# One attention and feed-forward block on one core: the steady steps in another order

## What is computed

```
x = x + tanh(g_xattn) * (context @ (Wv @ Wout) + bout)          # for these shapes
h = layernorm(x); s1 = 127 / max|h|;  h = round(h * s1) @ round(w1)  -> dequantised + b1
h = gelu(h)
h = layernorm(h); s2 = 127 / max|h|;  h = round(h * s2) @ round(w2)  -> dequantised + b2
x = x + tanh(g_ffn) * h
```

## Time and profile before

| | |
|---|---|
| median of 3 runs | 415.7 us (414.34 to 415.91) |
| the profiled execution, its own time | 413.45 us |
| its span, first to last instruction | 411.7 us |
| mean granted TensorE clock | 0.893 of full |
| busy: PE, DVE, ACT, POOL | 315.3, 299.3, 274.2, 268.2 us |

### The profile page before, as it was taken

How to read it: one execution, slowest core, us unless ns; L and a number is a source line. 1 busy time by engine, 2 the same in 40 slices (tenths; PEclk the granted TensorE clock), 3 DMA queues, 4 the chain that set the end, 5 groups by cost and what they waited for, 6 DMA issues and landing times. The chain is left out here.

```text
span 411.7 us, 5770 instructions
## 1 busy us (share of the span) xinstructions
PE 315.3 (77%) x1661; PEld 201.2 (49%) x1690; DVE 299.3 (73%) x520; ACT 274.2 (67%) x443; POOL 268.2 (65%) x298
## 2 busy tenths in 40 slices
PE   2976827759798989797979797989897666665553
PEld 2855516343556565555555554656464434332232
DVE  0168395978788989797979798979798858565710
ACT  2113672666878887878787888969695959594220
POOL 4052669386878887878787888787777868484100
PEclk9998987997989998989999999989898969695785
DMA  7665213325385756566665657490707161715173
GB/s 236 240 247 191 61 49 83 102 50 130 83 176 121 184 124 158 139 144 139 144 151 131 160 123 178 106 201 28 154 27 153 53 127 52 129 52 103 62 127 94
DMA packets 97974, 51.56 MB, mean 125 GB/s; under 512 B 86567, under 2 KB 88800, under 8 KB 97942
## 3 DMA queue, kind: packets, MB, share of 16 engines
q1 hardware_dynamic: 97046, 51.14, 50.6%
q10 hardware_dynamic: 896, 0.04, 0.1%
HBM read 21.78 MB, written 8.41 MB: 73 GB/s over the span
## 5 line engine op out<-in xcount | busy, mean ns | idle before, releaser
L343 POOL TENSOR_TENSOR y<-u,g_bc 128x1024 f32<-128x1024 f32 x64 | 151.4, 2368 | 41.5 <-ACT u L512 40.9
L681 DVE TENSOR_TENSOR y<-y,slot_c 128x1024 f32<-128x1024 f32 x64 | 77.8, 1216 | 47.3 <-PE slot_c L929 31.5
L968 PE MATMUL bank_f<-w2T,q2T 128*128 128x256 f16 x512 | 78.8, 308 | 9.9 <-DMA q2T<-q 7.6
L685 DVE TENSOR_REDUCE amax<-y 128x1 f32<-128x1024 f32 x64 | 77.6, 1213 | 1.8
L493 ACT ACTIVATE q<-y,scale 128x1024 f16<-128x1024 f32 x64 | 69.9, 1142 | 12.8 <-DMA q2T<-q 9.7
L520 ACT ACTIVATE junk<-u,usum 128x1024 bf16<-128x1024 f32 x64 | 73.5, 1149 | 2.1
L968 PEld LDWEIGHTS bank_f<-w2T,q2T 128*128 128x128 f16 x512 | 55.7, 109 | 29.9 <-issue 10.2
L512 ACT ACTIVATE u<-slot_a,d 128x1024 f32<-128x1024 f32 x32 | 35.4, 1107 | 38.3 <-PE slot_a L957 38.3
L929 PE MATMUL slot_c<-ln_rows,rows 128*128 128x512 bf16 x112 | 41.7, 447 | 16.2 <-ACT rows L503 8.9
L904 PE MATMUL slot_a<-wvo,ctxT 128*128 128x256 f32 x208 | 51.4, 380 | 0.0
L726 DVE SCALAR_TENSOR_TENSOR res<-bank_f,d,x 128x256 f32<-128x256 f32 x64 | 27.8, 476 | 19.2 <-PE bank_f L971 19.2
(11 more groups left out here) (113 smaller groups left out, 449.6 us busy)
## 6 DMA issues: line engine op xcount, KB each, us to landing
c_in<-in_ctx SPq DMA_DIRECT2D x16, 512.0 KB, 5.0
x_in<-in_x SPq DMA_DIRECT2D x16, 512.0 KB, 3.5
out<-res SPq DMA_DIRECT2D x32, 256.0 KB, 2.0
y<-in_L_ffn_w SPq DMA_DIRECT2D x2, 1024.0 KB, 9.1
u<-in_L_xattn_Wkv SPq DMA_DIRECT2D x2, 512.0 KB, 6.2
u<-in_L_xattn_Wout SPq DMA_DIRECT2D x2, 512.0 KB, 7.5
q2T<-q SPq DMA_TRANSPOSE x64, 3.3
g_bc<-in_L_ffn_ln_g SPq DMA_DIRECT2D x1, 512.0 KB, 4.5
```

The costliest lines, as they stand in the source:

```text
L343: nc.gpsimd.tensor_tensor(y[:, k % 3, t, :], u[:, t, :], g2_bc[:, :], ALU.mult).then_inc(gain2_done, 1)
L681: nc.vector.tensor_tensor(line, line, slot_c[:, :], ALU.add).then_inc(y_done, 1)
L685: nc.vector.tensor_reduce(amax[:, 1, t:t + 1], y[:, k % 3, t, :], AX.X, ALU.max, apply_absolute_value=True).then_inc(amax2_done, 1)
L968: nc.tensor.matmul(acc, q2T[:, t, j, :], w2T[:, j, :], start=(j == 0), stop=False)
```

## The change

No instruction is added or removed, and none changes its operands. The bodies of four engines are written in another order; POOL's stays.

- PE: `turn_context(i+3, 0)` moves from the head of body i to the end of the body before, `turn_context(i+3, 1)` behind `hidden(3)`. `second_product(i-3, 2)` goes ahead of `turn_rows`, `second_product(i-3, 3)` behind `correction(0)`, and `hidden(0)` follows at once; each later `hidden` has a `correction` ahead of it, and `second_product(i-2, 0)` goes ahead of `hidden(2)`. Half of the attention comes before `second_product(i-2, 1)`.
- ACT: tile 2 is quantised with tiles 0 and 1, ahead of the gelus; tile 3 stays behind the squares, where now the second half of the context is taken first. The first half is taken ahead of `take_rows`.
- DVE: `join` before the rows, `final(i-3, 2)` and `final(i-3, 3)` behind the first row.
- SP: the transpose of tile 2 a body earlier, behind `load_context`, and `store(i-2, 0)` behind it.

```diff
@@ SP
                 if live(i - 3):
-                    store(i - 3, 0)
-                    turn_second(i - 3, 2)
                     turn_second(i - 3, 3)
                 if live(i):
                     turn_first(i)
+                if live(i - 2):
+                    turn_second(i - 2, 0)
                 if live(i + 4) and i + 4 > 1:
                     load_x(i + 4)
+                if live(i - 2):
+                    turn_second(i - 2, 1)
+                if live(i - 3):
+                    store(i - 3, 1)
                 if live(i + 5) and i + 5 > 2:
                     load_context(i + 5)
                 if live(i - 2):
-                    turn_second(i - 2, 0)
-                    turn_second(i - 2, 1)
-                if live(i - 3):
-                    store(i - 3, 1)
+                    turn_second(i - 2, 2)
+                    store(i - 2, 0)
@@ ACT
-                    take_rows()
-                if 0 < i <= S:
-                    take_rows()
                 if live(i + 3) and i > 0:
                     take_context(i + 3, 0)
+                if 0 <= i <= S:
+                    take_rows()
                 if live(i - 2):
                     quantise(i - 2, 0)
                     quantise(i - 2, 1)
+                    quantise(i - 2, 2)
...
                 if live(i + 3) and i > 0:
                     take_context(i + 3, 1)
                 if live(i - 2):
-                    quantise(i - 2, 2)
                     quantise(i - 2, 3)
@@ DVE
+                    join(i + 2)
                 if live(i - 1):
                     row(i - 1, 0)
-                    if live(i + 2):
-                        join(i + 2)
-                    row_max(i - 1, 0)
...
                 if live(i - 3):
                     final(i - 3, 2)
                     final(i - 3, 3)
                 if live(i - 1):
+                    row_max(i - 1, 0)
+                    row(i - 1, 1)
@@ PE
-                if live(i + 3):
-                    turn_context(i + 3, 0)
+                    turn_context(4, 0)
+                if live(i - 3):
+                    second_product(i - 3, 2)
                 if i <= S + 1:
                     turn_rows()
                 if live(i - 1):
                     correction(i - 1, 0)
-                if live(i + 3):
-                    turn_context(i + 3, 1)
                 if live(i - 3):
-                    second_product(i - 3, 2)
+                    second_product(i - 3, 3)
+                if live(i):
+                    hidden(0)
...
                     hidden(3)
+                if live(i + 3):
+                    turn_context(i + 3, 1)
                 if live(i + 1):
                     shift_first(i + 1)
+                if live(i + 3):
+                    attention(i + 3, 0)
                 if live(i - 2):
-                    second_product(i - 2, 0)
                     second_product(i - 2, 1)
                 if live(i + 3):
-                    attention(i + 3, 0)
                     attention(i + 3, 1)
+                if live(i + 4):
+                    turn_context(i + 4, 0)
```

More of the change, by code:

```diff
@@ L549, in body @@
                     quantise(i - 2, 1)
+                    quantise(i - 2, 2)
+                if live(i):
+                    gelu(0)
+                    square(0)
+                    gelu(1)
+                    square(1)
+                    gelu(2)
+                    square(2)
+                    gelu(3)
+                    square(3)
                 if live(i + 3) and i > 0:
                     take_context(i + 3, 1)
-                if live(i):
-                    for t in range(T):
-                        gelu(t)
-                        square(t)
                 if live(i - 2):
-                    quantise(i - 2, 2)
                     quantise(i - 2, 3)
@@ L786, in body @@
                     statistics(i + 2, 3)
+                    join(i + 2)
                 if live(i - 1):
                     row(i - 1, 0)
-                    if live(i + 2):
-                        join(i + 2)
-                    row_max(i - 1, 0)
-                    row(i - 1, 1)
-                    row_max(i - 1, 1)
-                    if i == S:
-                        scales(slice(1, 2), slice(0, 2))
-                    row(i - 1, 2)
-                    row_max(i - 1, 2)
                 if live(i - 3):
@@ L801, in body @@
                 if live(i - 1):
+                    row_max(i - 1, 0)
+                    row(i - 1, 1)
+                    row_max(i - 1, 1)
+                if i == S:
+                    scales(slice(1, 2), slice(0, 2))
+                if live(i - 1):
+                    row(i - 1, 2)
+                    row_max(i - 1, 2)
                     row(i - 1, 3)
@@ L1030, in body @@
                 if live(i):
-                    hidden(0)
+                    hidden(1)
                 if live(i - 1):
                     correction(i - 1, 2)
+                if live(i - 2):
+                    second_product(i - 2, 0)
                 if live(i):
-                    hidden(1)
-                if live(i - 3):
-                    second_product(i - 3, 3)
+                    hidden(2)
                 if live(i - 1):
@@ L1040, in body @@
                 if live(i):
-                    hidden(2)
                     hidden(3)
+                if live(i + 3):
+                    turn_context(i + 3, 1)
                 if live(i + 1):
                     shift_first(i + 1)
+                if live(i + 3):
+                    attention(i + 3, 0)
                 if live(i - 2):
-                    second_product(i - 2, 0)
                     second_product(i - 2, 1)
                 if live(i + 3):
-                    attention(i + 3, 0)
                     attention(i + 3, 1)
+                if live(i + 4):
+                    turn_context(i + 4, 0)
             for i in bodies:
```

## The result

The changed kernel takes **390.19 us** (median of 4 runs, 389.86 to 393.29), the one before 415.81 us beside it: a ratio of 0.9401 with a 95% interval of 0.9348 to 0.9454. The profiled execution of the changed kernel is its slowest, 393.29 us with a span of 391.5; so the two traces differ by 20.2 us of span where the medians differ by 25.6.

The account below looks back on a forecast made before the run. A loop of waits through PE, ACT, POOL and DVE, no full engine, was taken to set the step. Savings of 14.9, 3.8, 1.4, 0.8 and 4.3 make 25.2 us off 413.45: 388.2, raised to 390; range 382 to 401.

Parts of the forecast that it names:

- The way from rows to gelu: PE and ACT, rows to first gelu: first product can start at T+6.63 (T: last square's end), 1.02 us sooner.
- The step: Steady step by the loop's sum, DVE's work or PE's work: 18.3 us, taken as 18.5, ends 17.7 and 19.6.
- The clock: PE in steady steps: full clock, since no single wait is over half a microsecond.
- rival A: Clock still falls in every steady step: 1.15 us each on eleven steps, 402 us; chance 0.14.
- rival B: Tile 2's q2T transpose lands late behind the context load, delaying `turn_rows`: 5.5 us over eleven steps, 396 us; chance 0.17.
- my own signs of being wrong: Steady steps: PE waits for q2T, clock averages 0.92, or a new wait over 1 us ahead of `hidden(0)`.
- Rival C: Tile 3's q2T transpose lands late ahead of `hidden(0)`: 7 us slower at a 6.5 us landing, 423 us; chance 0.03.
- Ten steps: From `quantise_first` of step 3 to that of step 13: 199.9 us become 185, saving 14.9 us.
- Fill: Steps 1 and 2: first product no longer behind the wait of `correction(1)`; 1.6 and 2.2, together 3.8 us saved.
- Step 13: Step with a nearly full PE before it: 19.9 becomes 18.5, 1.4 us saved.
- Late steps: Steps 14 and 15: clock falls anyway, only `correction(1)` leaves the path; 0.4 a step, 0.8 us saved.
- The drain: Program end: earlier tile 2 transpose 1.5, one last product instead of two 1.9, less tile 3 waiting 0.9; 4.3 us.

Follow-up runs that it names:

- the experiment with the queue turned: Tile 2's transpose put ahead of the context load, against the changed kernel with scales first and first-half store behind tile 3's transpose: 381.31 us, ratio 0.9148.
- the kernel with only the drain undone: Changed kernel, with tile 2's transpose of steps 14 and 15 back behind the first-half store: 392.22 us, ratio 0.9437.
- the last one: Changed kernel with scales first, store behind tile 3's transpose, tile 2's transpose ahead of the context load, and fills in bodies 14 to 18: 378.18 us.

## Why the prediction was right, point by point

**The way from rows to gelu.** Rows, correction and `row(0)` stand at T+4.46 to T+5.85, as in the earlier trace rows, to a hundredth of a microsecond. Tile 3's product starts at T+5.91 (5.65 by the sum), and the first product waits for q1T (forecast 0.2 to 0.3 us, shown 0.4). So `gelu(0)` starts at T+8.78, where the loop's sum has 8.5. Undoing two of the moves cost 0.45 and 0.58 us a step, as worked out; on the kernel before, the same product's move costs time.

**The step**: 18.3 by the sum, shown 18.27 to 18.3 where nothing disturbs it. The loop is the right one, but that its sum is right to a hundredth is luck. The scales ended 20.59 us behind T (20.44 counted), the first w1 product came 5.18 behind them (4.85), `gelu(0)` 1.28 behind that (1.50), and from there to the last square's end it was 9.57 (9.83, since no gelu waited for its product). The four errors cancel. The 0.2 that I added for crossings that I could not resolve was not there. The three ways to the sum were not of equal worth: DVE's and PE's idle times are small because they wait for the loop, and with the scales sooner the step goes to 18.02. I had also called DVE the busiest engine of both steps; in the slow-clock one PE is, with 18.17 us.

**The clock** stayed at 1.00 in the steady steps but one, as forecast, and rival A fell. But the reason that I gave, that no single wait is over half a microsecond, is not shown to be the cause. Filling the idle stretch of the kernel before keeps the clock; yet in the kernel with tile 2's product put back the stretch is idle for 1.28 us, and the clock stays too, as it does in the kernel before with the one move, where PE waits 1.31 and 0.87 us in a step and the context turn stands where it stood. With the load of x first, it held behind one wait of 2.54 us and fell behind another. What exactly lets it fall stays open.

The one step in which it did not stay is this, in the changed kernel's trace: the step, a DMA queue and the q1T transpose in its first microseconds, and PE at the first product and behind it:

```profile
162.01:183.54 21.53, 18.31 (x101) 11.29 (x100) 17.60 (x31) 16.86 (x27) 15.83 (x17) 0.92 0.66 135
...
q8 instruction: 1, 0.02, 1.7%
...
q1T<-q SPq DMA_TRANSPOSE x1, 4.9
...
168.91 0.59 PE L963 MATMUL slot_a<-w1T,q1T 128*128 128x512 f16 x2 [2.43 <-DMA q1T<-q]
...
170.16 1.06 PE L935 MATMUL slot_c<-ln_rows,rows 128*128 128x512 bf16 x2
```

The transpose landed 4.9 us after its issue in place of 3.1, PE waited 2.43 us, the clock went to 1.2 GHz behind it (granted 0.50 from 170 to 173 us), and the step took 21.5 us, 3.2 too long. This execution is 3.1 us above the median. In the kernel before q1T had 0.75 us or more to spare. The kernel with the late fills has the same order up to this step; there q1T landed after 4.5 us, PE waited 2.03 us, the clock stayed at 1.00 and the step took 19.72 us. So of the 3.2 us I estimate 1.4 to 1.8 for the wait, and the rest for the clock.

I overlooked what was in flight beside the late transposes. In both traces one packet of 0.02 MB on DMA queue 8, which the profile calls "instruction", moved within 5 us of the issue of this q1T. It is the same with tile 2 of the changed kernel: of its nine transposes behind a context load three have no such packet beside them and landed after 4.2 to 4.3 us; six have one and landed after 4.7 to 6.2, and five of these six are the ones that PE waited for in the steady steps. No transpose that SP issued singly in the trace of the changed kernel landed after more than 4.5 us without such a packet. Not every packet goes with a late landing, and no run moves the packets, so that they are the cause is not shown.

**SP's queue, rival B.** I had 0.1 to 2.3 us over for tile 2 and counted nothing. The trace shows five waits of PE for tile 2 in steady steps, of 0.19 to 0.85 us, 2.9 us in all; the experiment with the queue turned gives 1.5 us on medians. That is under the 5.5 us of its price. But "PE waits for q2T in steady steps" was one of my own signs of being wrong, and it came; so did, in the disturbed step alone, a wait of over 1 us ahead of `hidden(0)`. The third, a clock of 0.92 in the steady steps, did not. Rival C did not come: tile 3 landed in time until the scales went ahead of the results and pushed the store. Then it did bite, by 0.2 to 0.3 us a step.

**Ten steps**: 14.9 forecast, 13.2 in the trace with the disturbed step and 16.4 without its 3.2; 15.6 in the kernel with only the drain undone, whose ten steps are the same. **Fill**: 3.8 forecast, 3.2 shown, but not where I had it: between starts of `quantise_first` step 1 gave 0.2 us (1.6 forecast), step 2 gave 2.7 (2.2 forecast), and 0.3 were there ahead of step 1. **Step 13**: 1.4 forecast, 1.9 shown.

**Late steps**: 0.8 forecast for two, 0.02 shown for step 14. The term that failed is the clock's: I kept the time at which it comes back as in the kernel before, and it came back later, at 320.3, 5.8 us behind the first correction (4.1 before). The fills show what the clock costs there: 2.45 us in step 14.

**The drain**: 4.3 forecast, with step 15 1.9 shown and 1.9 undone. The 1.9 of the last product came: in the changed kernel PE is left with one. The other two terms, 1.5 and 0.9, failed. The rows are SP, ACT and PE of the changed kernel, and between them (397.24) PE of the kernel before at the product that answers to 377.37:

```profile
370.41 0.34 SPq L230 DMA_DIRECT2D out<-res  x1
370.84 4.04 SPq L224 DMA_TRANSPOSE q2T<-q  x3
...
374.27 1.15 ACT L495 ACTIVATE q<-y,scale 128x1024 f16<-128x1024 f32 x1 [3.49 <-DMA q2T<-q]
...
397.24 1.05 PE L968 MATMUL bank_f<-w2T,q2T 128*128 128x256 f16 x8 [0.97 <-DVE res L726]
...
377.37 1.89 PE L974 MATMUL bank_f<-w2T,q2T 128*128 128x256 f16 x8 [0.97 <-DVE res L732]
...
385.97 1.87 PE L974 MATMUL bank_f<-w2T,q2T 128*128 128x256 f16 x8 [2.45 <-DMA q2T<-q]
```

Measured from the start of step 15 (350.07 before, 331.76 now), the first transpose behind the store is issued at 39.1 us (39.3 before), and ACT waits for whichever tile is first there. The second product of step 15's tile 0 starts at 45.6 in place of 47.2: the 1.5 us came. But it and the next one ran at 1.2 GHz, 1.89 and 1.92 us where the kernel before took 1.05 and 1.04. So the last-but-one store and the transpose behind it came no sooner (issued at 51.0, before 50.7), and the last wait ends at 54.2, before at 54.1: nothing is left of the 1.5 and nothing came of the 0.9. The sum had not asked whether the clock would be lower there. Nor did it ask what the store between tile 2 and tile 3 costs: moved behind tile 3, it gives 6.7 us from step 15 on.

**The total.** Without the disturbed step's 3.2 us the terms are 3.2 for the fill, 16.4 for the ten steps, 1.9 for step 13, 0.0 for step 14 and 1.9 for the rest: 23.4 where 25.2 were forecast, and 413.45 - 23.4 is 390.05, the median of the changed kernel to 0.1 us. The 1.8 us that I had carried over from the difference between median and profiled run of before, for which no term of the change stands, were as large as what the terms were too high. That the forecast of 390 was met to 0.2 us is this chance; its mechanism and its largest term held, its late steps and drain did not. The range of 382 to 401 held with room; its upper end goes with steps of 19.0 us, where the text had 19.6 as the forecast's end.

## What to carry to other kernels

Write down for the waits of one loop when each input arrives, and not only which one ends last: behind the two waits that the profile named, this kernel had a third input 0.75 us behind, and with the first two gone that one sets the step. A piece of work moved into an idle stretch helps only if its own inputs are early enough: alone it delayed what stood behind it and cost 2.4%; with its quantising moved along it is worth 0.58 us a step. In a queue that carries out its entries in order, ask of each store who stands behind it while it waits, above all at the end of the program, where nothing covers it.

## What the runs showed that I had not expected

- A TensorE clock that holds can be bought with work that nobody needs: 5 idle-time matmuls a step gave 9.2 us on the kernel before, and fills in the last five bodies 6.4 us on the changed one.
- Step 14 takes 20.5 us in both orders, and 18.05 in the new order with the clock held.
- The first `quantise_first` of body 1 starts at 66.2 to 66.8 us in eight of the kernels and at 67.3 to 68.2 in six, though nothing ahead of it was edited: in the later ones PE waits 7.8 us in place of 5.4 for DVE ahead of the second weight sum. One execution of each kernel was traced, and the cause was not looked for. The kernel with the second correction put back, that with tile 2's product put back, the three with the scales first, and the last one are among the later ones, so 1 to 1.7 us of their times are not their edit's.
